# Turning stacked queries and keys by DMA, with three sequences in flight, in a language-model tower

## The reference, cut to what matters

```python
q = heads(h @ Wq[l] + bq[l]); k = heads(h @ Wk[l] + bk[l]); v = heads(h @ Wv[l] + bv[l])
a = band_attention(q, k, v, mask)        # each token attends to tokens within +-64
h = layer_norm(h + a @ Wo[l] + bo[l], ln1_s[l], ln1_b[l])
f = gelu(h @ W1[l] + b1[l])              # 192 -> 768
h = layer_norm(h + f @ W2[l] + b2[l], ln2_s[l], ln2_b[l])
```

## Time and profile before

| | |
|---|---|
| median of 3 runs | 7546.3 us (7543.4 to 7549.4) |
| the profiled execution | 7546.2 us |
| its span, first to last instruction | 7544.4 us |
| TensorE busy | 6561.0 us, 87% |
| VectorE busy | 4502.2 us, 60% |
| ACT busy | 2636.1 us, 35% |
| POOL busy | 1087.0 us, 14% |
| mean granted TensorE clock | 0.973 |

### The profile page before, as it was taken

How to read it: one execution, slowest core, us unless ns; L and a number is a source line. 1 busy time by engine, 2 the same in 40 slices (tenths; PEclk the granted TensorE clock), 3 DMA queues, 4 the chain that set the end, 5 groups by cost and what they waited for, 6 DMA issues and landing times. The chain is left out here.

```text
span 7544.4 us, 143226 instructions
## 1 busy us (share of the span) xinstructions
PE 6561.0 (87%) x53714; PEld 4915.5 (65%) x53714; DVE 4502.2 (60%) x11562; ACT 2636.1 (35%) x4677; POOL 1087.0 (14%) x1089
## 2 busy tenths in 40 slices
PE   1999999999999999999999999978888882399999
PEld 1777777777777777777777777756666662255665
DVE  6666666666666666666666666667766676522221
ACT  0444444444444444444444444433333330011111
POOL 4000000000000000000000000011111110233332
PEclk9999999999999999999999999999999995699999
DMA  5000000100000100000000000000000000122222
GB/s 99 15 14 14 14 14 14 29 14 14 14 14 14 29 14 14 14 15 15 25 18 14 14 14 14 14 29 15 15 17 17 15 16 8 29 55 54 54 57 42
DMA packets 194744, 173.32 MB, mean 23 GB/s; under 512 B 44402, under 2 KB 181268, under 8 KB 194644
## 3 DMA queue, kind: packets, MB, share of 16 engines
q1 hardware_dynamic: 166996, 139.45, 6.6%
q0 software_dynamic: 27648, 32.53, 2.9%
HBM read 113.75 MB, written 58.17 MB: 23 GB/s over the span
## 5 line engine op out<-in xcount | busy, mean ns | idle before, releaser
L682 ACT ACTIVATE pT<-bank 128x384 f32<-128x384 f32 x1920 | 857.9, 489 | 1184.2 <-PE bank L507 1184.2
L855 DVE TENSOR_REDUCE mx<-bank 128x2 f32<-128x384 f32 x1548 | 813.1, 554 | 497.2 <-PE bank L481 497.2
L479 PE MATMUL bank<-maskb,eyeb 128*128 128x384 bf16 x1932 | 642.7, 333 | 194.3 <-DVE mx L855 67.7
L576 PE MATMUL bank<-hT,w 96*128 96x256 f32 x3072 | 770.9, 387 | 43.5 <-ACT hT L702 43.5
L505 PE MATMUL bank<-maskb,eyeb 128*128 128x384 bf16 x1920 | 634.9, 331 | 53.6 <-ACT pT L682 49.2
L481 PE MATMUL bank<-kT,qT 128*128 128x192 bf16 (+2 forms) x3864 | 640.6, 248 | 0.0
L507 PE MATMUL bank<-qT,kT 128*128 128x192 bf16 (+2 forms) x3840 | 629.3, 246 | 0.0
L576 PEld LDWEIGHTS bank<-hT,w 96*128 96x128 f32 x3072 | 542.6, 190 | 125.4 <-ACT hT L702 72.6
L466 PE MATMUL bank<-eyeb,stack 128*128 128x128 bf16 x7728 | 518.3, 222 | 70.3 <-DVE stack L841 70.3
L466 PEld LDWEIGHTS bank<-eyeb,stack 128*128 128x128 bf16 x7728 | 467.6, 99 | 102.8 <-DVE stack L841 80.8
L588 PE MATMUL bank<-w,pT 128*128 128x192 f32 x3072 | 533.5, 330 | 0.0
(11 more groups left out here) (200 smaller groups left out, 11266.8 us busy)
## 6 DMA issues: line engine op xcount, KB each, us to landing
hcur<-hbuf SPq DMA_DIRECT2D x165, 192.0 KB
hbuf<-hout SPq DMA_DIRECT2D x128, 192.0 KB, 2.0
amb<-am_d SPq DMA_DIRECT2D x131, 128.0 KB, 2.9
exp_wg<-in_ewg SPq DMA_DIRECT2D x16, 576.0 KB
exp_wu<-in_ewu SPq DMA_DIRECT2D x16, 576.0 KB
exp_wd<-in_ewd SPq DMA_DIRECT2D x16, 576.0 KB
xs<-xr SPq DMA_DIRECT2D x32, 208.0 KB, 2.1
hbuf<-emb_z SPq DMA_DIRECT2D x17, 384.0 KB
```

What stands on the lines that cost most here:

```text
L479: nc.tensor.matmul(dst[:, 0:SCOLS], eyeb[:], maskb[:, masks, :], start=True, stop=False)
L576: last = nc.tensor.matmul(bank[s][f // 2][:, (f % 2) * S:(f % 2 + 1) * S], w1[:, c, f * P:(f + 1) * P], hT[s][:, c, :], start=(c == 0), st ...
L682: ph.inc(nc.scalar.activation(pT[s][:, h % NPT, :], bank[s][h % 2][:, 0:SCOLS], ACT.Exp, scale=SCALE), "p", s)
L855: last = nc.vector.tensor_reduce(mx[s][:, :, h], src[:, 0:SCOLS].rearrange("p (t k) -> p t k", t=T), AX, ALU.max)
```

## The change

**Turning.** The six fills and their copies are gone. `qT` and `kT` become the two halves of one buffer `qkT`, and SP turns the stack of each tile with one transposing DMA, two for a sequence, of 128 x 3072 bf16 each. They are issued when the stack is done and K, whose `qkT` has the same s, has finished its key-side scores.

**Three sequences.** A half now has a third member G, which is projected and stacked, while F, stacked one half earlier, gets its query-side scores and maxima, and K its back end. G has K's s. Since K's banks are in use, G's input transposes, q, k and v go to the banks of the other s (`bank[1 - s]`), and the front end's turned input gets a buffer of its own (`hTa`), as do the outputs (`oT`). There are 2 + 4 x 32 token halves and 34 causal ones. The weights of the front are needed one half earlier than before; the bias of the output projection gets its own buffer `vbo` and load.

**Back end between scores.** The third group of products, `unkept`, the output transposes, `att` transposes, projection and `h1` transposes stand at heads 2, 3, 4, 6, 8 and 11 of F's query-side scores (VectorE's parts of them at heads 4, 5 and 8 to 10), and all up-projections follow the transposes of the maxima.

The diff, cut to its core:

```diff
-Turn = namedtuple("Turn", "s it pair wf wb")
+Turn = namedtuple("Turn", "s it pair wf wb wo")
-TOK_PLAN = Plan(input=1, qk=3, proj=2, v=6, h1=8, up=9, res=1, stats=2, mean=2, center=3, norm=4)
-CAUSAL_PLAN = Plan(input=0, qk=1, proj=2, v=12, h1=10, up=12, res=2, stats=3, mean=4, center=5, norm=6)
-LAG = 2
+TOK_PLAN = Plan(input=1, qk=3, prod=(6, 10), last=2, unkept=3, out=4, v=5, att=6, proj=8, h1=11,
+                sums=4, vadd=5, res=8, stats=8, mean=8, center=9, norm=10)
+CAUSAL_PLAN = Plan(input=1, qk=2, prod=(6, 10), last=2, unkept=None, out=4, v=5, att=6, proj=8, h1=11,
+                   sums=4, vadd=5, res=8, stats=8, mean=9, center=10, norm=10)
...
-        qT = sbs("qT", [P, NH, S], BF16)
-        kT = sbs("kT", [P, NH, S], BF16)
+        qkT = sbs("qkT", [P, 2 * NH, S], BF16)
+        qT = [x[:, 0:NH, :] for x in qkT]
+        kT = [x[:, NH:2 * NH, :] for x in qkT]
+        oT = sbs("oT", [P, 3 * S], F32)
...
-        def pe_scores1(ph, pe, F, h, masks, qcols):
+        def pe_scores1(ph, pe, F, G, h, masks, qcols):
             s = F.s
             if h == 0:
-                ph.wait(pe, "ev_v", s, F.it)
-                ph.wait(pe, "ev_s", s, F.it)
+                ph.wait(pe, "xp", s, F.it)
+            if h == 1 and G:
+                ph.wait(pe, "qk", G.s, G.it)
             if h >= 3:
                 ph.wait(pe, "mx", s, F.it, h - 2)
...
-        def tensor_half(ph, pe, F, K):
+        def tensor_half(ph, pe, G, F, K):
...
+            for h in range(NH):
+                if K:
                     pe_scores2(ph, pe, K, h, masks, kcols)
+                if G and h == plan.input:
+                    if causal and F:
                         ph.wait(pe, "sT", F.s, F.it, 0)
+                    ph.wait(pe, "x0" if causal else "h_in", G.s, G.it)
+                    ph.inc(pe_transposes((h1 if causal else hcur)[G.s], bank[1 - G.s][0]), "hT_ps", G.s)
+                if G and h in (plan.qk, plan.qk + 1):
+                    pe_qk(ph, pe, G, h - plan.qk)
+                if K and h in plan.prod:
+                    pe_products(ph, pe, K, F, plan.prod.index(h), kcols)
+            for h in range(NH):
+                if F:
+                    pe_scores1(ph, pe, F, G, h, masks, qcols)
+                if K and h == plan.last:
+                    pe_products(ph, pe, K, F, 2, kcols)
+                if K and h == plan.unkept:
+                    pe_unkept(ph, pe, K)
+                if K and h == plan.out:
                     pe_output(ph, pe, K)
+                if G and h == plan.v:
+                    pe_v(ph, pe, G, F, bank3_key)
+                if K and h == plan.att:
                     pe_att_T(ph, pe, K)
                 if K and h == plan.proj:
                     pe_project(ph, pe, K)
                 if K and h == plan.h1:
                     pe_h1_T(ph, pe, K, xr if causal else h1)
             if F:
                 pe_maxima(ph, pe, F)
             if K:
+                for f in range(FSC if causal else FC):
+                    up(ph, pe, K, f)
                 (pe_shared_down if causal else pe_down)(ph, pe, K)
...
+            if G:
+                s = G.s
+                sc = Chain(ph, dve, G, "sl")
+                dve_qk(ph, dve, G)
...
+                dve_stack(ph, dve, sc, G, kb[:, NT:NT + T] if causal else kb[:, bass.ds(G.pair * (NST * T) + s * T, T)])
+            if F and not causal:
+                s = F.s
+                ph.wait(dve, "am_in", s, F.it)
+                ph.inc(nc.vector.tensor_tensor(wam[s][:], window[:], amb[s][:].unsqueeze(1).to_broadcast([P, T, S]),
+                                               ALU.mult), "wam", s)
...
             for h in range(NH):
                 if F:
                     dve_row_max(ph, dve, F, h, qcols)
+                if K and h == plan.sums:
+                    dve_sums(ph, dve, bc, K, None if causal else amc[:, bass.ds(K.pair * (NST * T) + K.s * T, T)])
+                    dve_divide(ph, dve, bc, K, not causal)
+                    if not causal:
+                        dve_add_unkept(ph, dve, bc, K)
+                if G and h == plan.vadd:
...
+                    dve_v(ph, dve, G)
...
+                def transposes(ph, G, K):
+                    s = G.s
+                    if K:
+                        sp.lower_val(ph.value("sc2", K.it))
+                    ph.wait_apart(sp, "stk", s, G.it, None, c_in, 96)
+                    if K:
+                        ph.wait(sp, "sc2", K.s, K.it)
+                    sp.wait_ge(c_in, 96)
+                    for t in range(T):
+                        ph.inc(sp.dma_start_transpose(qkT[s][:, :, t * P:(t + 1) * P],
+                                                      stack[s][:, t].rearrange("p w h k -> p (w h k)")), "xp", s)
...
-                        loads(Turn(1, it, i, None, None))
-                        store(Turn(0, it, i, None, None))
-                        loads(Turn(0, it + 1, i + 1, None, None))
-                        store(Turn(1, it, i, None, None))
+                        loads(turn(1, it, i))
+                        transposes(tok, turn(0, it + 1, i + 1), turn(0, it, i))
+                        store(turn(0, it, i))
+                        loads(turn(0, it + 1, i + 1))
+                        transposes(tok, turn(1, it + 1, i + 1), turn(1, it, i))
+                        store(turn(1, it, i))
                     it = l * PAIRS + (PAIRS - 1)
-                    loads(Turn(1, it, PAIRS - 1, None, None))
+                    sp.lower_val(tok.value("qk", it))
+                    tok.wait_apart(sp, "v", 1, it, None, c_in, 96)
                     tok.wait(sp, "qk", 1, it)
-                    tok.wait(sp, "v", 1, it)
+                    sp.wait_ge(c_in, 96)
                     load_front(l + 1)
-                    store(Turn(0, it, PAIRS - 1, None, None))
+                    loads(turn(1, it, PAIRS - 1))
+                    load_bo(l + 1)
+                    transposes(tok, turn(0, it + 1, 0), turn(0, it, PAIRS - 1))
+                    store(turn(0, it, PAIRS - 1))
```

More of the change, by code:

```diff
@@ L448, in pe_v @@
                                             wqkv[:, c, 2 * D:3 * D], start=(c == 0), stop=(c == 1))
             ph.inc(last, "v_ps", s)
[L451 to L458, removed]
-                ph.wait(pe, "ev_v", s, F.it, 1)
-            if f == 5:
-                ph.wait(pe, "ev_s", s, F.it, 1)
-            dst = bank[s][f % 4][:].bitcast(BF16)
-            side, h0 = f // 3, (f % 3) * 4
-            for j in range(4):
-                for t in range(T):
-                    last = nc.tensor.transpose(dst[:, j * S + t * P:j * S + (t + 1) * P],
-                                               stack[s][:, t, side, h0 + j, :], eyeb[:])
-            ph.inc(last, "fill", s)
@@ L515, in pe_products @@
                 ph.wait(pe, "v", s, K.it)
+            if g == 2 and F:
+                ph.wait(pe, "v", F.s, F.it)
             ph.wait(pe, "p", s, K.it, 4 * g + 4)
@@ L794, in dve_qk @@
             s = F.s
+            o = 1 - s
             if F.wf is not None:
@@ L1050, in pool_half @@
                     ph.inc(nc.gpsimd.tensor_tensor(rstd[s][:], ve[s][:], half[:], ALU.pow), "rstd2", s)
-                else:
-                    input_rstd(ph, pool, s, K.it + 1)
+            if F and causal:
+                input_rstd(ph, pool, F.s, F.it + 1)
         def token_layers(eng, half_of):
-            half_of(tok, eng, Turn(0, 0, 0, 32, None), None)
+            first = Turn(0, 0, 0, 32, None, 16)
+            half_of(tok, eng, first, None, None)
+            half_of(tok, eng, first._replace(s=1), first, None)
@@ L1145, in _ @@
                 load_front(0)
+                load_bo(0)
                 for s in ST:
@@ L1215, in sync_half @@
                         load_h(F.it + 1, s)
+                    if G:
+                        s = G.s
+                        if K:
+                            sp.lower_val(ph.value("sc2", K.it))
+                        ph.wait_apart(sp, "stk", s, G.it, None, c_in, 16 * 7)
+                        if K:
+                            ph.wait(sp, "sc2", K.s, K.it)
+                        sp.wait_ge(c_in, 16 * 7)
+                        for t in range(T):
+                            ph.inc(sp.dma_start_transpose(qkT[s][:, :, t * P:(t + 1) * P],
+                                                          stack[s][:, t].rearrange("p w h k -> p (w h k)")), "xp", s)
                     if K:
```

225 lines of the change are left out of this document (95 added, 130 removed).

## The result

The changed kernel takes 7729.8 us (7724.4 to 7732.9) beside 7547.5 for the kernel before: a ratio of 1.024 [1.022, 1.026], 2.4% slower. The prediction said 7431, with a range of 7280 to 7700.

A forecast was written before the change was run, and what follows sets the result against it. TensorE, busy 87% of the span, was taken as the bound. From 7546 us: token halves -132, layer changes +25, prologues +12, causal halves -20, sum -115, giving 7431 us; 8-in-10 range 7280 to 7700.

The forecast's parts named there:

- the clock term: Token halves: one fall of TensorE's clock in most, 3.4 us at 1.2 GHz, costing 1.0 us as a mean.
- its causal counterpart: Causal halves: two long waits each; 1.0 us added for falls, where falls took 0.87 before.
- The sum without falls: Redrawn token half at full clock: 35.25 against 37.28 us, 2.03 less, with 3.3 us of new idle.
- Causal halves: Causal stage redrawn: 36.6 us against 38.2 at full clock, -1.6; with 1.0 for falls, -20 us over 31 halves.
- the likeliest case: Whole kernel: 7431 us, chance 0.50; its own range 7330 to 7510 from drawing error and both clock bounds.
- The signs: If right: 3 us idle before h1's transposes, token halves about 36.2, clock near 0.95, no DMA wait, one weight wait per layer.
- Transposing DMAs: SP's turning of stacks: 10 to 20 us a sequence, 33 us free to hide them, steady halves' cost nothing.
- The rival from the Trainium skill: Transposing DMAs at 1309 ns per 128x128: forty-eight take 63 us, kernel near 11,700; DMAs outlasting the half had chance 0.15.
- Layer changes: Four layers: projection needs new weights one half earlier, loaded behind the store; stack's chain moves by 6.3 us; +25 us.
- Prologues: Start of both stages: exposed transposing DMAs and a second stack, +4 us each with 10 us DMAs, +14 with 20; +12 taken.
- The clock stays up: Rival, chance 0.15: no falls; token halves -260, layer changes and prologues +37, causal halves -35; 7290 us.
- The clock stays down: Rival, chance 0.15: two falls, 6.9 us, on maxima, up and down in token halves, 3.4 us lost each; 7760 us.

The follow-up runs named there:

- e5_busy_front: Changed kernel with filling matmuls where TensorE waited, plus SP's load of the next layer's front weights moved ahead of the store: 7298.6 us, 0.967 of before.
- e2_front: Changed kernel with SP's load of the next layer's front weights moved ahead of the previous pair's store, no filling matmuls: 7649.7 us, 1.012 of before.
- e3_pool: Changed kernel with GpSimd's addition of the second bias to h1 held until the maxima are rounded, no filling matmuls: 7647.8 us, 1.016 of before.
- e4_twice: Changed kernel with each transposing DMA issued twice, the first time into a spare buffer, no filling matmuls: 7674.3 us, 1.021 of before.

## Why the prediction was wrong

- **The step that failed is the clock term**, "I expect one fall in most halves ... 1.0 us as a mean (bounds: 0, and 1.7 for one whole fall)", and its causal counterpart "I add 1.0". In the token stage the number of falls was right: 102 of the 127 halves have one low stretch of 3.4 us. Their price was not. Of the 3.4 us, 2 to 2.5 were put on maxima and up-projections; in the half shown all of it lies there, and a steady half lost 1.62 us, nearly the upper bound (0.62 x 127 = 79 us more than forecast). Two low stretches in one half cost no more than one here (37.52 and 37.54 us). Falls at the layer changes took another 16. In the causal stage the term was far too small: I let the 0.87 of before stand and added 1.0, and 5.42 is 3.55 more, 110 us in 31 halves. These halves had waits of 2.4 and 2.8 us where those of the earlier trace rows had one of 1.8. Most spent 13.7 us at the lower clock, in the half shown 10.2 of it in one stretch on maxima, gating and up-projections. This term had no bounds at all. Together the clock is 205 of the 299 us between 7431 and 7729.8.
- **The sum without falls was too short as well**, by some 95 us. A steady token half was drawn as 35.25 us and takes 35.92 at full clock, 0.67 more; that is 85 us, and the layer changes add 15. The idle stretch came as drawn (3.23 for 3.3), but all stands later: output transposes start 13.5 us into the half shown (drawn 13.2), those of `h1` 23.65 (23.1), those of the maxima 25.4 (24.4); what follows takes 10.6 at full clock (10.85). About 0.46 of the 0.67 is L843, which I copied from the earlier trace rows without GpSimd's addition beside it. With the clock term right, the forecast would have been near 7640, slower than before.
- **Causal halves**, drawn 36.6: 36.51 at full clock.
- **The range.** The bounds of the likeliest case, 64 us of drawing either way and 0 to 1.7 of clock, add up to 7240 to 7585; I wrote 7330 to 7510. The measured time lies 145 us above even the wider one, as the causal clock had no bound in it.
- **The signs** came almost all: 3.2 us of idle ahead of `h1` released by VectorE, a token clock of 0.94, no wait of scores on DMA in steady halves, one wait at each layer change. They did not tell a faster kernel from a slower one; only the length of the half (38.0 for 36.2) did.
- **Transposing DMAs**, "cost in steady halves is nothing": right, and shown by doubling them. Each landed 5.5 us after its issue, and the second is issued 3.8 us behind the first, so a sequence takes about 9.3 us, just under the 10 to 20 that I took. The Trainium skill, "Advanced Engine Details and Errata", section "X-Bar Transpose (TRN2)", gives 350 to 400 GB/s, by estimate 4 us a sequence; the trace is slower, with 3.8 us of issue for each half of it. The rival from the Trainium skill, "VectorE: DVE Perf Modes", section "The three transpose paths" (1309 ns for a 128x128), doesn't hold here: one DMA that turns 24 such tiles took 5.5 us, 0.23 for each.
- **Layer changes**, +25: 30.1 of waits, and with what follows them the halves there cost 40 us more than before at full clock (37.8 by e5_busy_front), 56 with the falls. **Prologues**, +12: 7.9, 8.0 and -3.1 at the ends of the stages, 12.8.
- **The rivals.** "The clock stays up" is 7290, and the experiment that holds it up gives 7336. That is closer than its terms deserve: token halves were 95 us too short in it, layer changes included, and causal ones 44 us too long (-35, where they gave -79). "The clock stays down" has 7760, near the measured time by luck: it loses 3.4 us in a token half and nothing in the causal stage, where the trace has 1.62 and 5.42. Its condition, 4.1 us of low clock on maxima, up- and down-projections, was not met in the half shown, which has 3.4.

Not settled: why falls settle into one of two patterns in the causal stage, and why the clock stays low for 10.2 us there while TensorE is busy. Both vanish with the idle stretches. Nor is it known how much idle time makes a fall here: 1.4 us made none, 1.8 us made one in some halves and 3.2 us in every half.

## What to carry to other kernels

Taking work from a busy TensorE can cost time: count the longest idle stretch that the new schedule leaves, and price the clock on the work right behind it; 3.2 us of idle in 37.5 cost 1.6 us, and two waits of 2.4 and 2.8 in a causal half 5.4. Before giving up on such a change, fill the stretch with matmuls that nobody reads: it tells in one run what the schedule is worth. Then move real work there, all of the chain and not only its head; two waits of 1.4 and 0.7 us did no harm. While a clock falls in some halves, small edits can't be priced, since each shifts the falls (e2_front, e3_pool, e4_twice); make the clock steady first.

## What was not expected of the hardware

- A VectorE operation on 128x24 took 0.67 us in place of 0.18 while a GpSimd addition of 128x384 (1.00 us) ran.
- One transposing DMA of 128x3072 bf16 holds SP's queue for 3.8 us and lands 5.5 us after its issue.
- Behind its idle stretches TensorE stayed at the lower clock (0.50 granted) for 10.2 us though busy without a gap, over the maxima, the gating and most of the up-projections of a causal half.
- Causal halves of one program text took either 39.73 or 41.93 us on average, by the pattern of their falls; the two patterns make 68 us in an execution, and executions of one kernel came out 55 to 73 us apart.
